# Heads of 64 in a four-layer attention and FFN kernel: values unfolded, outputs transposed in 64x64 parts of the array, output projection in two parts summed in PSUM

## The reference

```python
q = x @ Wq; k = context @ Wk; v = context @ Wv          # each split into 16 heads of 64
sim = einsum('bhid,bhjd->bhij', q, k) * 64 ** -0.5
attn = softmax(sim, axis=-1)
out = einsum('bhij,bhjd->bhid', attn, v)                # heads side by side again: [.., 1024]
return out @ Wo + bo                                    # 1024 -> 128
```

## Time and profile before

| | |
|---|---|
| median of 3 runs | 4117.2 us (4113.91 to 4119.01) |
| the profiled execution | 4117.64 us |
| its span | 4115.9 us |
| TensorE busy in the span | 3653.7 us, 89% |
| VectorE | 2844.3 us, 69% |
| ScalarE | 1929.6 us, 47% |
| GpSimd | 1099.0 us, 27% |
| mean granted TensorE clock | 0.956 |

### The profile page before, as it was taken

One profiled execution on the slowest core, in us unless ns is written; L12 is line 12 of the kernel. 1 busy time (PEld: TensorE's weight loads), 2 busy tenths in 40 slices (PEclk: granted clock), 3 DMA queues, 4 the chain that ended last, 5 costly groups with the idle time before them and its releaser, 6 DMA issues. The chain is left out here.

```text
span 4115.9 us, 108620 instructions
## 1 busy us (share of the span) xinstructions
PE 3653.7 (89%) x42378; PEld 3001.4 (73%) x42378; DVE 2844.3 (69%) x6136; ACT 1929.6 (47%) x4763; POOL 1099.0 (27%) x1214
## 2 busy tenths in 40 slices
PE   5999699978887788789999988869999997999999
PEld 4887688876666644478887865548887886888888
DVE  5777555559999899856665668876665665666665
ACT  2454455547777744345555531115554553323232
POOL 1222133332222233212222223322222221232322
PEclk9999899989999999989999998889999998999999
DMA  1000000000000000000000000000000001000000
GB/s 68 9 9 6 24 0 0 0 10 9 10 9 9 7 1 0 4 24 6 8 6 8 6 9 0 0 22 6 8 6 9 6 6 31 1 10 10 0 10 11
DMA packets 14699, 39.25 MB, mean 10 GB/s; under 512 B 3277, under 2 KB 4749, under 8 KB 12814
## 3 DMA queue, kind: packets, MB, share of 16 engines
q1 hardware_dynamic: 14341, 33.95, 2.7%
HBM read 29.74 MB, written 4.19 MB: 8 GB/s over the span
## 5 line engine op out<-in xcount | busy, mean ns | idle before, releaser
L641 ACT ACTIVATE projL<-bank 128x512 f32<-128x512 f32 (+1 forms) x640 | 373.3, 604 | 714.7 <-PE bank L126 698.9
L464 POOL TENSOR_TENSOR probL<-probL,invL 128x1024 f32<-128x1024 f32 x160 | 304.7, 1904 | 1274.6 <-DVE invL L723 1274.6
L1153 POOL TENSOR_TENSOR accM<-accM,partM 128x512 f32<-128x512 f32 x272 | 347.6, 1278 | 816.2 <-DVE partM L1255 814.8
L1226 ACT ACTIVATE siluM<-bank 120x512 f32<-120x512 f32 x240 | 143.5, 598 | 456.4 <-PE bank L126 456.2
L321 ACT ACTIVATE probL<-bank,neg_maxL 128x64 f32<-128x64 f32 x1024 | 304.9, 325 | 110.0 <-PE bank L285 107.5
L545 PE MATMUL bank<-valuesL,probTL 64*64 64x128 f32 x10240 | 321.0, 275 | 13.1 <-ACT probTL L651 13.1
L545 PEld LDWEIGHTS bank<-valuesL,probTL 64*64 64x64 f32 x10240 | 282.0, 134 | 68.9 <-issue 54.2
L720 DVE TENSOR_REDUCE totalL<-probL 128x16 f32<-128x1024 f32 x160 | 194.9, 1218 | 196.6 <-ACT probL L656 196.4
L712 DVE TENSOR_REDUCE neg_maxL<-bank 128x16 f32<-128x1024 f32 x160 | 195.9, 1224 | 187.4 <-PE bank L564 142.8
L1175 PEld LDWEIGHTS bank<-downT,hM 120*128 120x128 f32 x2560 | 310.5, 192 | 15.0
L1175 PE MATMUL bank<-downT,hM 120*128 120x128 f32 x2560 | 311.5, 275 | 0.0
(11 more groups left out here) (253 smaller groups left out, 8990.0 us busy)
## 6 DMA issues: line engine op xcount, KB each, us to landing
ct0L<-in_ctxP SPq DMA_DIRECT2D x24, 192.0 KB, 2.4
ct1L<-in_ctxP SPq DMA_DIRECT2D x24, 192.0 KB, 3.1
x<-in_x SPq DMA_DIRECT2D x4, 1024.0 KB, 8.8
out<-x SPq DMA_DIRECT2D x4, 1024.0 KB, 3.9
nct<-in_ctxT SPq DMA_DIRECT2D x16, 192.0 KB, 2.5
w_natural<-in_L0w SPq DMA_DIRECT2D x2, 1152.0 KB, 8.7
downT<-in_L3down SPq DMA_DIRECT2D x1, 1200.0 KB, 11.9
gateT<-in_L3gate SPq DMA_DIRECT2D x1, 900.0 KB, 4.7
```

Of the source, the lines that this page charges most:

```text
L464: nc.gpsimd.tensor_tensor(segments(prob[:, slot, :]), segments(prob[:, slot, :]), per_segment(inv[:, slot, :]), ALU.mult).then_inc(prob_re ...
L641: nc.scalar.activation(proj[:, u, :], rot.bank(step, f"P{u}")[0:rows, :], ACT.Copy, scale=scale if paired and u % 2 == 0 else 1.0).then_in ...
L1153: nc.gpsimd.tensor_tensor(acc[:, :, :], acc[:, :, :], part[:, ex % 2, :, :], ALU.add)\
```

## The change

L2 and L3 get a function of their own, `paired_attention`; L0 keeps `wide_attention`, L1 `narrow_attention`. What is different from the paired case of before:

- There is no fold. wq, wk, wv and wo are each split into a high and a low part. Values are `context @ wv`, 64 wide for each head: two fills of a bank a step (V0, V1), each 2 x 3 matmuls of 256 columns; ScalarE keeps V0, VectorE V1.
- `output` has the values stationary and the transposed probabilities moving, 64x64 parts with 64 columns. It gives the output transposed, two heads side by side on 128 rows, in two banks. It no longer sums over steps: ScalarE copies it out as `oT_hi` (`keep_output`), VectorE takes the rest as `oT_lo` (`split_output`), one step later.
- `project_out`, three steps behind, multiplies by wo in 12 matmuls of 256 columns (three for each pair of heads and half of the tokens), summed in bank 4 over the group. `keep_sum` copies the sum out once a group (ScalarE, step 2), `turn_output` transposes it back with 4 transposes (TensorE, step 3), `add_output` adds it to x (VectorE, step 3). `finish` moves to step 0, two groups behind.
- Banks 5 to 7 turn among P, T and V.

```diff
+        o_bank, sum_bank = c.psum[:, 2:4, :], c.bank[4]
+        xt_bank, y_bank = c.bank[0], c.bank[1]
+        a, b_, c_ = c.bank[5:8]
+        bank = {"P0": a, "P1": b_, "T0": c_, "T1": a, "P2": b_, "P3": c_, "V0": a, "V1": b_}
...
+                def value(k, slot, half):
+                    cols = slice(4 * k * dh, 4 * (k + 1) * dh)
+                    weights = hi["wv"][:, cols], lo["wv"][:, cols]
+                    for u in range(2):
+                        tok = slice((2 * half + u) * P, (2 * half + u + 1) * P)
+                        last = product(nc, bank[f"V{half}"][:, u * 4 * dh:(u + 1) * 4 * dh],
+                                       (ct_hi[slot][:, tok], ct_lo[slot][:, tok]), weights)
+                    last.then_inc(V_done, 1)
...
+                def output(v_slot):
+                    for p in range(2):
+                        for u in range(2):
+                            for b in range(2):
+                                for h in range(2):
+                                    for t in range(2):
+                                        col = (4 * p + 2 * u + b) * SEQ
+                                        last = nc.tensor.matmul(
+                                            o_bank[h * SEQ:(h + 1) * SEQ, t, col:col + SEQ],
+                                            values[t * SEQ:(t + 1) * SEQ, v_slot, 2 * u + b, 2 * p + h, :],
+                                            probT[t * SEQ:(t + 1) * SEQ, 4 * h + 2 * p + u, b * SEQ:(b + 1) * SEQ],
+                                            start=True, stop=True)
+                    last.then_inc(O_done, 1)
+
+                def project_out(n, k):
+                    pe.wait_ge(oT_lo_kept, n + 2)
+                    for p in range(2):
+                        cols = slice((2 * k + p) * P, (2 * k + p + 1) * P)
+                        for t in range(2):
+                            out = sum_bank[:, t * 2 * P:(t + 1) * 2 * P]
+                            part = slice(p * 2 * P, (p + 1) * 2 * P)
+                            for step, (w, o) in enumerate(((hi, oT_hi), (lo, oT_hi), (hi, oT_lo))):
+                                last = nc.tensor.matmul(out, w["wo"][:, cols], o[:, t, part],
+                                                        start=(k == 0 and p == 0 and t == 0 and step == 0),
+                                                        stop=(k == Q - 1 and p == 1 and t == 1 and step == 2),
+                                                        skip_group_check=True)
+                    if k == Q - 1:
+                        last.then_inc(sum_done, 1)
```

TensorE's step k of group i, with m = i * Q + k:

```diff
+                        pe.wait_ge(V0_kept, m + 1)
+                        projection(k, slot, 0)
+                        pe.wait_ge(V1_kept, m + 1)
+                        projection(k, slot, 1)
+                        if older:
+                            pe.wait_ge(P_kept, 4 * m + 4)
+                            transposed_probs(m - 2, 0, k % 2)
+                            pe.wait_ge(P_kept, 4 * m + 5)
+                            transposed_probs(m - 2, 1, k % 2)
+                        pe.wait_ge(P_kept, 4 * m + 6)
+                        projection(k, slot, 2)
+                        if oldest:
+                            if k == 3:
+                                pe.wait_ge(sum_kept, i + 1)
+                            project_out(m - 3, (k + 1) % Q)
+                        if k == Q - 1:
+                            pe.wait_ge(S_read, m + 1)
+                            transpose_group(nc, pe, c, xt_bank, i + 1, xh_ready, xt_done)
+                            if started(i, 1):
+                                turn_output(i - 1)
+                        if older:
+                            pe.wait_ge(T_kept, 2 * m + 1)
...
+                        projection(k, slot, 3)
+                        if older:
+                            pe.wait_ge(T_kept, 2 * m + 2)
+                        value(k, slot, 0)
+                        pe.wait_ge(P_kept, 4 * m + 8)
+                        pe.wait_ge(S_read, m + 1)
+                        if k == Q - 1:
+                            pe.wait_ge(xT_ready, i + 2)
+                            if started(i, 1):
+                                pe.wait_ge(out_read, i)
+                        if older:
+                            pe.wait_ge(oT_lo_kept, m - 1)
+                        value(k, slot, 1)
+                        if older:
+                            output((k - 2) % 4)
+                        scores(slot, k)
```

ScalarE's and VectorE's:

```diff
+                        keep_projection(m, 0)
+                        keep_projection(m, 1)
+                        if older:
+                            keep_probs(m - 2, 0)
+                        if k or started(i, 1):
+                            exponentials(m - 1, (k - 1) % 2)
+                        if older:
+                            keep_probs(m - 2, 1)
+                        keep_projection(m, 2)
+                        if k == 2 and started(i, 1):
+                            keep_sum(i - 1)
+                        if k == Q - 1:
+                            keep_transposed(nc, act, c, xt_bank, i + 1, 1 - slot, xt_done, xT_ready)
+                        keep_projection(m, 3)
+                        keep_value(m, k)
+                        if older:
+                            keep_output(m - 2)
...
+                        if k == 3 or started(i, 1):
+                            split_output(m - 3)
+                        if k or started(i, 1):
+                            maxima(m - 1, (k - 1) % 2)
+                        if k == Q - 2:
+                            normalise_group(nc, dve, c, i + 1, xh_ready, xt_done)
+                        if k == 0 and started(i, 2):
+                            finish(i - 2)
+                        if k or started(i, 1):
+                            totals(m - 1, (k - 1) % 2)
+                        if k == Q - 1 and started(i, 1):
+                            add_output(i - 1)
+                        keep_value(m, k)
+                        if k == Q - 1:
+                            split_transposed(nc, dve, c, i + 1, 1 - slot, xT_ready, xT_split)
...
-                (narrow_attention if layer == "L1" else wide_attention)(c, layer, **ATTENTIONS[layer])
+                KINDS[layer](c, layer, **ATTENTIONS[layer])
```

239 lines of the change are left out of this document (237 added, 2 removed).

## The result

| | before | after |
|---|---|---|
| median | 4116.4 us (4113.9 to 4119.0) | 4149.6 us (4144.9 to 4152.0) |
| the profiled execution, its span | 4117.6, 4115.9 | 4148.5, 4146.7 |
| granted TensorE clock, mean | 0.956 | 0.955 |

After takes 1.0079 of before (95% interval 1.0062 to 1.0097): 0.8% slower. The forecast was 4133, or +0.4%, slower, in a range of 4090 to 4165.

A forecast was written before the change was run, and what follows sets the result against it. It took TensorE as today's bound, with a cross-engine chain only 0.65 us short of it that binds after the change. Per layer 5.2 - 7.1 + 9.6 = +7.7; two layers +15.4 on 4117.6 gave 4133 us, range 4090 to 4165.

The forecast's parts named there:

- The steps: Inside a group in L2 and L3: the cross-engine chain from output to next output sets 9.42, 9.42, 9.90, 10.2 us.
- rival 4: TensorE's value and output-projection matmuls: 256 columns cost as much as 512, steps 11.5 us, total 4375; chance 0.07.
- TensorE as the bound: Attention steps: TensorE's own work stays the limit, groups 2.2 us shorter, total 4053; chance 0.10.
- rival 3: Loop edges: more matmuls add a 3.4 us low-clock stretch at each of 12 edges, 20 us, total 4153; chance 0.13.
- same: Whole program: outcome counted as unchanged, 4109 to 4125 us; chance 0.19.
- slower: Whole program: outcome of the changed kernel taking longer than before; chance 0.62.
- The start: Layer start: the fold goes, first projection 7.0 us after the weights instead of 14.1, -7.1 us a layer.
- The first two steps: First two steps of a layer: no older output to handle, about -1.6 us a layer.
- The edges: Loop edges: VectorE's links run under TensorE's 4.75 us idle, -0.5 us at each of 6 edges a layer.
- The end: Last scores to layer end: the longer tail of output work costs +9.6 us a layer, bounds +7 and +14.
- P0 to first scores: Layer start, from first projection to first scores: no change, 0 us.
- the steady groups: 15 groups a layer: 38.94 us each against 38.29, +0.65 us a group.

The follow-up runs named there:

- The double split: Changed kernel with VectorE's split of the output issued twice in every step, the first into an unread spare tile; 4287.0 us, 1.0417 of the kernel before.
- the run with both late: Changed kernel, VectorE's split behind maxima and subtraction, TensorE's output projection behind P3, ScalarE's sum and x copies behind P3's; 4097.6 us, 0.9954 of before.
- The run with GpSimd later: Changed kernel with GpSimd splitting the second context tile only after VectorE's split of x; 4143.4 us, 1.0064 of the kernel before.
- before + 32: Kernel before with 32 identity transposes on TensorE at the very start of L2 and L3; 4130.6 us, 1.0035 of the kernel before.
- the run with the maxima first: Changed kernel with maxima and subtraction ahead of the split in VectorE's queue, TensorE's order unchanged; 4181.2 us, 1.0160 of the kernel before.

## Why the prediction was right, point by point

**The steps: right, and by the mechanism named.** Forecast 9.42, 9.42, 9.90, 10.2; measured 9.41, 9.41, 9.90, 10.23 in both layers. Rung by rung from the start of output: copy 1.17 forecast, 1.23 measured; split 2.22, 2.28; maxima 3.41, 3.43; subtraction 4.67, 4.68; exponentials 5.94, 5.93; probabilities 6.89, 6.90; P2 kept 7.37, 7.38; second value block 8.51, 8.50; next output 9.42, 9.41. The double split shows that this chain sets the steps. The two prices that no row of before had came out at 0.12 us from one 256-column matmul to the next (0.12 taken) and 1.02 for the copy (1.05 taken). The reason given against rival 4, that the columns make the time in all rows from 128 to 512, is only half right: 128-column transposes start 0.109 us apart (the prediction read 0.10 off a block of eight), 256-column matmuls 0.12, 512-column ones 0.23. From 128 to 256 the columns hardly count. The 256-column ones stay above the 0.107 us that the prediction estimated as their floor. A group costs +0.67 us (forecast +0.65).

**The rivals.** TensorE as the bound did not come; the run with both late shows what it needed. 256 columns at the price of 512 is refuted. Larger edges did not come in after: 88.2 and 90.5 us for the six edges of L2 and L3 against 88.6 and 96.3. But an edge can grow by 4 us without any instruction more in the loop, by its idle time; rival 3 had priced its growth as one more stretch at half clock. Such a longer stretch does come, at five of after's twelve edges and two of before's, and costs 0.8 to 1.4 us each. A slip without weight: the chances of "same" and "slower" add to 0.17 and 0.64 by their own shares, where 0.19 and 0.62 are given.

**The size: +31 instead of +15.** The forecast's direction and its steps came by the reason given; that the total fell into the range owes something to terms that were off both ways. By the terms of the sum, both layers together:

- *The start*, -14.2 forecast, -9.6 measured. The step that failed is "three more splits 1.14 apart": that pitch came from a row where GpSimd was still. In L3 the four took 8.3 us to the next operation instead of 4.6. The run with GpSimd later shows a part of it, 3.2 us.
- *The first two steps*, -3.2 forecast, +0.3 measured: from the first to the second scores the clock is still low for a part (mean 0.81 and 0.79), 9.28 and 9.40 us where before took 7.89 at full clock. In other runs without filler it is 7.7 in some layers, so this term changes from run to run by up to 1.7 us a layer.
- *The edges*, -6.0 forecast and -6.2 measured, but as -0.3 and -5.8. The cover that was argued did come: edges with a granted clock of 0.88 or 0.89 take, without their idle time, 11.0 to 11.1 us in before and 10.5 to 10.7 in after, 0.45 less each, some -5.3 for twelve. The other two parts nearly cancel: 4.0 us less idle time, all in L3, where before + 32 shows that it goes with the place of the code, and 3.1 more from longer stretches at half clock. The argument held; that the sum did too is luck.
- *The stops in L3*, not foreseen, +4.8 (seven steps of 9.91 to 10.24 instead of 9.41).
- *The end*, +19.2 forecast, +21.9 measured. Up to the last split (19.8 forecast, 19.7 measured from the last scores) it holds; then the output projection goes at half clock, 0.21 a matmul, its sum is turned at half clock too, and the last statistics end at 27.6 instead of 26.6. The forecast also took L3's end of before (17.0 us) for both layers, and L2's was 16.1.
- *P0 to first scores*, 0 and +1.2 (granted clock 0.50 in both layers, where before had 0.64 and 0.67); *the steady groups*, +19.5 and some +21; the rest of the program, 0 and -2.9.

**And the comparison itself.** After is slower than before by 10.4 and 9.8 us between first and last scores with both as built, by 7.9 in L2 with 32 transposes in each, and by 33.7 in L3 with them. The sign holds at each of these four places; the size 0.8% is that of two particular places of code. It wouldn't hold across places: L2 of after as built (643.6) is faster than L2 of before + 32 (659.5). What no shift touches is the group inside a pass, 38.96 against 38.29 us, and 15 times that difference, 10 us, is what the two layers as built show.

## What to carry to other kernels

Where two engines' queues are written out by hand, follow one product around until it comes back to the same engine: the length of that ladder is the step, and a new link on it is paid in full even if each engine looks idle enough. Moving one operation out of it only helps if no queue that waits for it holds up the rest, as the run with the maxima first and the run with both late show together. And before a difference of some tenths of a per cent is put down to an edit, shift the code by a few KB and time it again: 32 idle transposes moved these two kernels by 15 and 38 us.

## What was not expected of the hardware

- The time of a loop of 2576 (before) or 2784 (after) recorded TensorE instructions depends on where its code lies: 12.6 to 20.2 us from scores to scores at an edge, idle 3.4 to 7.9 of it, and stops of mostly 0.5 to 1.5 us inside dense 64x64 blocks (128 instructions in 1.04 us). Shifts by 16, 32 and 64 KB changed a layer by less than 2 us, 4 and 8 KB by up to 26 us (8 KB once by only 3.7).
- A step can be lengthened by the clock as well as by the chain: with the split doubled, waits of 1.1 to 1.2 us were followed in 19 of 126 steps by an output at a granted clock of 0.50, 1.99 us instead of 1.16.
- VectorE and GpSimd hold each other up in SBUF-to-SBUF work, mostly by turns: the 1024-wide split 1.21 alone, 1.65 to 2.29 together (1.21 once); GpSimd's 512-wide operations 1.04 and 1.27 alone, mostly 2.02 to 3.15 together.
- At the start of a layer of after TensorE's granted clock was 0.50 for 9.0 us after 14.7 to 15.2 us of idling, and 1.00 when it had worked until 1.77 us before. In other runs it rose sooner after 13.3 to 15.4 us of idling (8.2 to 8.5 us to the first scores, mean 0.54 to 0.56).
